# A Mamba scan with softplus as one ScalarE activation in place of a hand-made series, and a new timetable for its first batch

## The reference

```python
hidden = _rmsnorm(residual, norm_w)
xz = hidden @ W_in
x, z = jnp.split(xz, 2, axis=-1)
xc = conv1d(x)                      # 4 taps, depthwise, causal
x = jax.nn.silu(xc + conv_b)
x_dbl = x @ W_x
dt = jax.nn.softplus(x_dbl[..., :DT_RANK] @ W_dt + b_dt)
Bm, Cm = x_dbl[..., DT_RANK:DT_RANK + D_STATE], x_dbl[..., DT_RANK + D_STATE:]
A = -jnp.exp(A_log)
def step(h, inp):                   # scanned over the 224 positions
    x_t, dt_t, B_t, C_t = inp
    dA = jnp.exp(dt_t[..., None] * A)
    h = dA * h + (dt_t * x_t)[..., None] * B_t[:, None, :]
    y = jnp.einsum('bdn,bn->bd', h, C_t)
    return (h, y)
y = (ys + x * D) * jax.nn.silu(z)
out = residual + y @ W_out
```

## Time and profile before

| | |
|---|---|
| median of 3 runs | 3511.4 us (3509.2 to 3520.05) |
| span of the profiled execution | 3514.3 us |
| scan phase, first scan to last | 85.0 to 1932 us |
| VectorE busy, 300 to 1650 us | 1271.8 of 1350 us |
| TensorE busy, 300 to 1650 us | 1206.8 of 1350 us |
| ScalarE busy, 300 to 1650 us | 1083.6 of 1350 us |
| GpSimd busy, 300 to 1650 us | 1115.4 of 1350 us |

### The profile page before, as it was taken

How to read it: one execution, slowest core, us unless ns; L and a number is a source line. 1 busy time by engine, 2 the same in 40 slices (tenths; PEclk the granted TensorE clock), 3 DMA queues, 4 the chain that set the end, 5 groups by cost and what they waited for, 6 DMA issues and landing times. The chain is left out here.

```text
span 3514.3 us, 59833 instructions
## 1 busy us (share of the span) xinstructions
PE 3186.9 (91%) x20864; PEld 2223.5 (63%) x20864; DVE 2650.7 (75%) x4673; ACT 2396.1 (68%) x5339; POOL 1805.3 (51%) x1211
## 2 busy tenths in 40 slices
PE   5699889888889888988998899999999999899999
PEld 4566556665566556655665566666666666578887
DVE  2889999999999999999987576777777777523222
ACT  5778887778787887778774477776777677632222
POOL 2677887888787878888786100100000010055554
PEclk8899999999999999999999999999999999999999
DMA  5566666766677666666576121211211121120010
GB/s 164 154 180 183 185 167 164 199 185 163 156 193 192 164 161 184 177 183 158 157 201 182 53 71 49 83 55 47 75 64 47 52 81 66 43 77 25 27 46 24
DMA packets 286298, 425.03 MB, mean 121 GB/s; under 512 B 28753, under 2 KB 226129, under 8 KB 281394
## 3 DMA queue, kind: packets, MB, share of 16 engines
q1 hardware_dynamic: 278637, 411.44, 42.0%
q10 hardware_dynamic: 7365, 9.77, 1.0%
HBM read 320.12 MB, written 101.02 MB: 120 GB/s over the span
## 5 line engine op out<-in xcount | busy, mean ns | idle before, releaser
L811 POOL TENSOR_TENSOR a_hs<-a_rep,a_bmat 128x896 f32<-128x896 f32 x512 | 1061.5, 2097 | 294.6 <-PE a_yps L323 294.4
L443 ACT ACTIVATE a_states<-a_rep,a_a_neg 128x224 f32<-128x224 f32 x2048 | 793.7, 438 | 98.0 <-DVE a_hs L707 96.4
L700 DVE TENSOR_TENSOR_SCAN a_states<-a_states,a_hs 128x900 f32<-128x900 f32 x384 | 779.7, 2031 | 73.8 <-ACT a_states L443 58.5
L1424 DVE CUSTOM_DVE_ANT_0 b_sc<-sps,early_mask 112x375 f32<-112x375 f32 x1024 | 500.3, 545 | 171.7 <-PE sps L1171 162.1
L1311 ACT ACTIVATE b_sc<-b_sc,b_nmax 112x750 f32<-112x750 f32 x512 | 467.3, 913 | 2.5 <-DVE b_nmax L1430 2.5
L1185 PEld LDWEIGHTS b_tps<-ident,b_sc 112*125 112x125 f32 x3072 | 362.2, 191 | 157.4 <-issue 126.1
L1564 POOL TENSOR_SCALAR b_x_var<-mv 112x2 f32<-112x2 f32 x16 | 3.4, 214 | 857.4 <-DVE mv L1475 857.4
L345 PE MATMUL a_work<-early_scan_hT,w_in 128*128 128x224 f32 x2048 | 427.6, 364 | 10.0 <-issue 7.2
L345 PEld LDWEIGHTS a_work<-early_scan_hT,w_in 128*128 128x128 f32 x2048 | 397.9, 197 | 51.1 <-issue 43.4
L707 DVE TENSOR_TENSOR a_hs<-a_states,a_cmat 128x896 f32<-128x896 f32 x384 | 419.2, 1092 | 13.2
L1185 PE MATMUL b_tps<-ident,b_sc 112*125 112x112 f32 x3072 | 410.7, 283 | 16.3 <-DVE b_pT L1438 14.9
(11 more groups left out here) (199 smaller groups left out, 5012.4 us busy)
## 6 DMA issues: line engine op xcount, KB each, us to landing
a_rep<-du_scratch SPq DMA_DIRECT2D x512, 224.0 KB, 5.7
w_in<-W_in_dram SPq DMA_DIRECT2D x128, 512.0 KB, 4.4
du_scratch<-early_du SPq DMA_DIRECT2D x16, 1792.0 KB, 11.4
ctx<-ctxT_dram SPq DMA_DIRECT2D x48, 500.0 KB, 5.8
v_scratch<-kv_out SPq DMA_DIRECT2D x96, 250.0 KB
k_scratch<-kv_out SPq DMA_DIRECT2D x96, 250.0 KB, 4.4
b_keys<-k_scratch SPq DMA_DIRECT2D x8, 1500.0 KB, 9.2
b_v<-v_scratch SPq DMA_DIRECT2D x8, 1500.0 KB
```

Of the source, the lines that this page charges most:

```text
L443: e = act.activation(rows(states[:, g % DA, :])[:, q, 1:ROW], rep[tile % REPS][:, j, 0, :], ACT.Exp, scale=a_neg[:, g % SLOTS, q:q + 1])
L700: dve.tensor_tensor_scan(state if g % G4 else whole, state, whole, 0.0, ALU.mult, ALU.add).then_inc(S["scan"], 1)
L811: pool.tensor_tensor(hs[g % RING][:, :, 1:ROW], rep[tile % REPS][:, j, 1, :].unsqueeze(1).broadcast_to([P, Q, L]), bmat[b % 2][:], ALU.mul ...
L1424: dve.tensor_tensor_reduce(out=sc[buffer_of(block)][:, j, cols], in0=sps[0:TT, j, 0:HALF], in1=mask[:, block % 2, cols], scale=-1.0, scala ...
```

## The change

The softplus of a pair becomes one activation with the function Softplus, read from PSUM and written to dt. All four pairs of a batch stand in one ACT step, with a table load ahead (placed by the build in front of the first of them) and one behind, back to the set with Exp and Ln. The series on VectorE, the sum on GpSimd, their constants and semaphores are gone. The PSUM bank of a pair is now free after its activation. In all three tables the four products of `dt_raw` move: LATER from slots -30, -28, -26, -24 to -30, -30, -29, -28, with the softplus at -28. In FIRST `skip`, `spread`, `u` and `store_du` move to earlier slots; the slots of batch 0's z steps stay.

```diff
-            "silu_x": [-43], "x_dbl": [-42], "xd": [-41], "store_bc": [-41], "dt": spaced(-40, 1), "parts": spaced(-39, 1),
-            "series": spaced(-38, 1), "logs": spaced(-37, 1), "skip": [-32, -31], "spread": [-28], "dt_sum": [-30],
-            "silu_z": [-20], "u": [-28], "store_du": [-27]}
+            "silu_x": [-43], "x_dbl": [-42], "xd": [-41], "store_bc": [-41], "dt": [-40, -40, -40, -39], "softplus": [-39],
+            "skip": [-38, -38], "spread": [-37], "silu_z": [-20], "u": [-38], "store_du": [-36]}
...
-            "x_dbl": [-33], "xd": [-32], "store_bc": [-32], "dt": spaced(-30, 2), "parts": spaced(-29, 2),
-            "series": spaced(-28, 2), "logs": spaced(-27, 2), "skip": [-20, -19], "spread": [-19], "dt_sum": [-18],
+            "x_dbl": [-33], "xd": [-32], "store_bc": [-32], "dt": [-30, -30, -29, -28], "softplus": [-28],
+            "skip": [-20, -19], "spread": [-19],
...
             def dt_raw(b, pair):
-                bank = take_bank(("dt", b, pair), "part", PAIRS * b + pair + 1)
+                bank = take_bank(("dt", b, pair), "dt", PAIRS * b + pair + 1)
...
-            def softplus_parts(b, pair):
-            def softplus_log(b, pair):
+            def softplus(b):
+                for pair in range(PAIRS):
+                    act.wait_ge(S["dt_ps"], PAIRS * b + pair + 1)
+                    act.activation(dt[:, 2 * pair:2 * pair + 2, :], pair_of_tiles("dt", b, pair),
+                                   ACT.Softplus).then_inc(S["dt"], 1)
+                act.preload_act_table_set("natural_log_exp_and_others")
...
-            def softplus_series(b, pair):
...
-            def softplus_sum(b):
...
             def scale_x(b):
                 pool.wait_ge(S["skip"], 2 * (b + 1))
-                pool.wait_ge(S["dt"], b + 1)
+                pool.wait_ge(S["dt"], PAIRS * (b + 1))
```

More of the change, by code:

```diff
@@ L221, in mamba_phase @@
             "bc0", "bc1", "du_out", "rep0", "rep1", "rep2",
-            "a_exp", "const", "log_small", "squares", "guess", "gain", "h", "res", "hT_ps", "hT", "x_ps", "z_ps",
-            "tap", "conv", "z", "xs", "zs", "xd_ps", "xd", "bc", "dt_ps", "log_part", "square", "part",
-            "dt", "skip", "u", "dA", "dbx", "scan", "hc", "hc_pool", "y_ps", "y", "gated", "o_ps", "sum", "wsum",
+            "a_exp", "const", "squares", "guess", "gain", "h", "res", "hT_ps", "hT", "x_ps", "z_ps",
+            "tap", "conv", "z", "xs", "zs", "xd_ps", "xd", "bc", "dt_ps", "dt", "skip", "u", "dA", "dbx", "scan", "hc", "hc_pool", "y_ps", "y", "gated", "o_ps", "sum", "wsum",
             "stats", "next_in", "next_bq", "next_wo", "next_v", "next_stats", "next_var", "next_log", "next_guess", "next_rstd", "next_ln",
@@ L234, in mamba_phase @@
         n_weights = 11
-        n_const = 6
+        n_const = 4
         def spaced(first, step):
@@ L250, in mamba_phase @@
             "older_taps": spaced(2, 2), "z": spaced(1, 2), "keep_z": spaced(2, 2), "residual": [9], "silu_x": [9],
-            "x_dbl": [10], "xd": [11], "store_bc": [11], "dt": spaced(12, 1), "parts": spaced(13, 1),
-            "series": spaced(14, 1), "logs": spaced(15, 1), "skip": [18, 19], "spread": [17], "dt_sum": [20],
-            "silu_z": [21], "u": [21], "store_du": [22]}
+            "x_dbl": [10], "xd": [11], "store_bc": [11], "dt": [13, 13, 14, 15], "softplus": [15],
+            "skip": [18, 19], "spread": [17], "silu_z": [21], "u": [21], "store_du": [22]}
         LATER = {
@@ L569, in wait_for_room @@
             def wait_for_room():
-                for name, value in (("xd_ps", B), ("dt_ps", PAIRS * B), ("hT_ps", 2 * B), ("z_ps", PAIRS * B), ("dt", B),
-                                    ("u", B), ("part", PAIRS * B), ("gated", B - 1), ("du_out", 16 * B),
+                for name, value in (("xd_ps", B), ("dt_ps", PAIRS * B), ("hT_ps", 2 * B), ("z_ps", PAIRS * B),
+                                    ("u", B), ("dt", PAIRS * B), ("gated", B - 1), ("du_out", 16 * B),
                                     ("kv_out0", 16 * UNITS // OUTS), ("kv_out1", 16 * UNITS // OUTS),
@@ L638, in scalar_program @@
                     keep_xd(b)
[L639 to L642, removed]
+                for b, _ in due(slot, "softplus"):
+                    softplus(b)
                 for b, _ in due(slot, "silu_z"):
@@ L762, in vector_program @@
                     dve.tensor_scalar(a_neg[:], a_neg[:], -1.0, None, ALU.mult).then_inc(S["const"], 1)
-                    dve.wait_ge(S["log_small"], 1)
-                    steps.after(dve.tensor_scalar(log_small[:], log_small[:], -1.0, None, ALU.mult))
-                    steps.settle()
                 for b, pair in due(slot, "older_taps"):
                     older_taps(b, pair)
-                for b, pair in due(slot, "series"):
-                    softplus_series(b, pair)
                 for b in range(B):
@@ L859, in gpsimd_program @@
                     gains(b)
-                for b, _ in due(slot, "dt_sum"):
-                    softplus_sum(b)
                 for b, _ in due(slot, "u"):
```

12 lines of the change are left out of this document (1 added, 11 removed).

## The result

The changed kernel takes 3544.6 us (median of 4 runs, 3541.9 to 3551.8); the kernel before, run beside it, 3510.3. The ratio is 1.0095 with an interval of [1.0078, 1.0112]: slower by about 34 us, where 3550 was forecast. The profiled execution's span is 3539.9 us, 25.6 more than that of before; it is that of the fastest of the changed kernel's four runs (3541.9), so part of the distance between 25.6 and 34 is the spread of the runs.

A forecast was written before the change was run, and what follows sets the result against it. VectorE, 94% busy, was taken to set the scan phase's pace. 43 us lost in windows 1 to 14, less 3 for batch 1 and 1 for batch 0, gave +39 us: 3550 us, own range 3530 to 3568, 8-in-10 range 3500 to 3588.

The forecast's parts named there:

- the walk: Window 4, from slot 7's product on VectorE to slot 10's scan: terms sum to 16.8 us, scan 10.1 us late.
- unit: TensorE's unit of keys and values between third and fourth pair: 5.68 us at half clock after idling, against 3.54.
- the weight piece and its read: ScalarE, before the decays of slot 10: sum of a weight piece 0.62 us and a read of 0.19.
- one of 9 to 12 us: Expected sign: one VectorE wait per window before slot 10's scan, released by ScalarE's decays, and no other new one.
- no slow clock: Rival: TensorE's keys-and-values unit takes 3.54 us, loss 1.0 a window, +10 us in all, 3521 us; chance 0.13.
- What VectorE gets back: After slot 10's scan: series pairs 3.5, wait before the last 1.7, slot 15 0.8, slot 21 1.0; 7.0 us.
- The 1.0 us for GpSimd in slot 21: VectorE's wait for GpSimd's late 4.0 us sum goes away, 1.0 us gained per window.
- the others catch up: Rival: other engines run ahead during VectorE's stall, remaining decay waits go, unit at full speed; 3493 us; chance 0.12.
- the net loss: Windows 1 to 14: 10.1 us late less 7.0 got back, 3.1 us lost each, 43 us in all.
- The second slow stretch: Rival: TensorE's clock also falls after the second output projection, 1.7 us a window, 24 more, 3574 us; chance 0.14.
- The switch: ScalarE table load priced 1.28 us alone; rival: 2 to 3 us more a window, about 3588 us; chance 0.06.
- no earlier: Batch 0: z's weight loads behind the store of du on SyncE's queue, so z gains nothing; batch 0 gains 1 us.

The follow-up runs named there:

- Experiment 7: Changed kernel plus 14 additional TensorE products over 128 rows ahead of the third pair's own products, batches 2 to 15: 3538.9 us, ratio 1.0092.
- experiment 2: Changed kernel with Relu in place of Softplus and no table loads around the step: 3489.5 us, ratio 0.9933 to the kernel before.
- Experiment 5: Changed kernel with the weights of the last two pairs of z issued ahead of the store of du: 3534.5 us, ratio 1.0079.
- experiment 4: Changed kernel with the third pair's products made seven times over from batch 2 on, to hold TensorE's clock: 3580.8 us, ratio 1.0191.

## Why the prediction was right

**The stall, by its terms.** From the product's end to the scan of slot 10 the walk gave 16.8 us and the trace has 16.2 (609.32 - 593.09). Each term: decays 1.56 (1.55 said), load 1.28, softplus 0.54 (0.53), unit 5.28 (5.68), sum 1.74, pair 1.02, softplus 0.55, load 1.28, copy 0.83, the weight piece and its read 0.6, decays 1.55. Only the unit was off by more than 0.2 us, by 0.4. Counted from slot 8, the scan of slot 10 is late by 9.3 to 9.6 us in windows 4 to 13, where 10.1 was said. It shows on VectorE as two waits rather than one: the add of slot 9 waits for the sum first. The prediction looked for one of 9 to 12 us and only for decays; the sum of states stands in the same row of TensorE, so it had to be expected as a releaser.

**The slow clock.** The unit ran 5.28 us after 5.94 us of idle time, at a clock of 0.50 in its first 3.4 us, as a row like it in the kernel before had the earlier trace rows. Experiment 7 took the idle time away and it ran 3.55. The rival "no slow clock" is out. But the idle stretch is not all of the story: in window 4 of the changed kernel the clock had fallen already when the third pair ran, ahead of the stretch (its two products took 1.43 us instead of 1.02):

```profile
589.22 1.43 PE L357 MATMUL a_work<-a_xd,early_w_dt 65*128 65x224 f32 x4 [1.67 <-ACT kv_out L484]
```

The rival's price was wrong too: taking the slow clock away brought at most 6 us of 34, not 29, since another slow stretch took its place.

**What VectorE gets back.** Slots 10 to 15 gave back 6.0 to 6.9 us (6.0 said). The 1.0 us for GpSimd in slot 21 did go, but the wait for decays in slot 22 rose from between 0.3 and 0.6 us to 1.7: that term was worth nothing. And 1.5 to 1.6 us that were not forecast (2.5 in window 4) came from the waits of slots 29, 1 and 4, which vanished in windows 4 to 13: the part of the rival "the others catch up" that came true. So the net loss in windows 4 to 13 was 1.6 us on average and not 3.1; in windows 1 to 3, where those waits stayed, it was 4.5 on average. Summed: windows 1 to 3, 13.5 us; 4 to 13, 16.1; window 14, 1.5; in all 31 where the prediction had 43.

**The second slow stretch** is there (the row below; TensorE idled 2.95 us before it) but cost 0.6 to 0.7 us a window and not 1.7, if what experiment 2 gained in slot 22 is put down to it. As a rival it had the mechanism right and its price wrong.

```profile
627.35 3.21 PE L317 MATMUL a_yps<-a_hs,a_fold 128*32 128x224 f32 x32 [2.95 <-DVE a_hs L671]
```

**The switch.** Loads take 1.28 us with 0.01 to 0.02 us on either side, and two of them 2.6 to 2.7 us in experiment 2. The drain of some 1.38 us per switch that the Trainium skill (ScalarE: Activation LUTs, "What ACT_TABLE_LOAD costs") adds is not seen. Its other statement (ScalarE activation tables: per-element evaluation and per-set limits, "What a function is on this engine"), that the function does not change the price, agrees within 2%: Softplus 544 ns, Relu 533 ns in experiment 2, 531 in the earlier trace rows.

**The first two batches.** Batch 1's softplus step was short as forecast, its fourth pair 1.08 us late; window 0 became 6.4 us shorter, where 3 was taken from a range of 0 to 9. The first scan came at 85.8 instead of 85.0, so batch 0 lost 0.8 where it was to win 1 (range 4.4 won to 3 lost). The reason was named and then priced at nothing: the weights of z behind the store of du were to bring z "no earlier", and they brought its third pair later, at 68.58 us after a wait of 16.42. Experiment 5 shows that this order cost 7.9 us of the first scan.

**The sum.** 31 - 6.4 + 0.8 = 25 us, the span's 25.6; 39 was forecast. By the medians the kernel is 34 us slower; that this is nearer to 39 is the spread of the runs and no merit of the sum. Two sizes were off in the same direction: the net loss of a later window, 1.5 us too high for windows 4 to 13, and the gain of window 0, 3.4 us too low; windows 1 to 3, 1.4 us above the forecast each, and the first scan made up for a part. So the mechanism was right, and its net by the spans was forecast half as large again as it came out (39 against 25.6). ScalarE's saving was 122 us, not 149.

## What to carry to other kernels

An engine that works strictly in order should not be given one step that needs several results, when one of these results needs that step's own first output to free a buffer: the step then lasts as long as the whole round, here 11.7 us where its own loads and activations take 4.5. Look in the timetable for what stands between the producers of the step's inputs; here, one unit moved by one slot turned 1% slower into 2% faster. And where one engine has no idle time at the end of a period, a gain earlier in the period can vanish: read where the same wait is back before counting it.

## What the hardware showed unexpectedly

Products over 65 of 128 rows, back to back, did not bring the clock back: in experiment 4 TensorE is at work in every us from 712 to 722, the granted clock stays at 0.50, and x28 took 10.82 us. In window 4 of the same run x28 such products took 5.57 us at a clock of 1.00. In experiment 7 the products over 128 rows, at the same place of the window and after 1.52 us of idle time, began at a falling clock too, but it came back while they ran:

```profile
582.00:584.00 2.00, 1.03 (x3) 0.85 (x4) 1.97 (x3) 1.03 (x3) 2.00 (x2) 0.70 0.74 143
584.00:586.00 2.00, 2.00 (x7) 1.53 (x6) 1.97 (x2) 1.43 (x4) 2.00 (x2) 0.50 0.62 131
586.00:588.00 2.00, 2.00 (x11) 1.70 (x10) 2.00 (x2) 1.12 (x3) 2.00 (x2) 0.94 1.00 283
```

Whether the number of rows or what went before makes the difference was not separated; that the products over 65 rows ran at the upper level in window 4 speaks against the rows alone.

The same sum of states after the same 2.02 us of idle time ran at either level, 1.74 us in one kernel and 3.20 in another, with seemingly the same work before it. What decides that stays open.
